# Convolution A three images ahead, the prologue's DMAs on three queues, and another order of the last convolutions

## The reference

```python
x = x + _L0_conv_ref(_gn(x), L0_conv_weights, L0_conv_biases)   # 3x3 convolution, zero padding, bias
x = x + _L1_conv_ref(_gn(x), 5)          # Newton-Schulz inverse of each 128x128 matrix, 5 iterations
x = x + _L2_conv_ref(_gn(x), L2_conv_weight)                    # 3x3 convolution, circular, by FFT
x = x + _L3_conv_ref(_gn(x), L3_conv_K)  # 3x3 convolution, last row and column set to zero
```

## Time and profile before

| | us |
|---|---|
| median of three runs | 725.62 (724.13 to 728.28) |
| the profiled execution | 727.48 |
| its span | 725.70 |
| busy: PE, weight loads | 607.9 (84%), 507.1 (70%) |
| busy: DVE, ACT, POOL | 533.2 (73%), 383.5 (53%), 198.6 (27%) |
| mean granted clock of PE | 0.954 |

### The profile page before, as it was taken

The page is one execution under the profiler, slowest core; times in us unless marked ns, Lnnn a source line. Parts: engine busy times, 40 slices in busy tenths (PEclk is TensorE's granted clock), DMA queues, the critical chain, the costliest instruction groups (busy, mean ns, idle before and its releaser), DMA issues.

```text
span 725.7 us, 11297 instructions
## 1 busy us (share of the span) xinstructions
PE 607.9 (84%) x3752; PEld 507.1 (70%) x3752; DVE 533.2 (73%) x1304; ACT 383.5 (53%) x559; POOL 198.6 (27%) x289
## 2 busy tenths in 40 slices
PE   0695679749989989899899989999999969995956
PEld 0464667748777777778778778778777858884644
DVE  3855976666796878797797779887978687648551
ACT  0351437424666566664667456656677436753632
POOL 5122023112252224231242315222423122201302
PEclk9998999969999999999999999999999998998888
DMA  5186001950379322971488334942372135222352
GB/s 152 54 106 186 1 30 34 148 182 30 90 82 268 75 81 52 158 209 44 101 85 255 86 85 71 237 121 64 75 241 53 35 80 168 53 74 70 85 132 58
DMA packets 89124, 76.43 MB, mean 105 GB/s; under 512 B 6572, under 2 KB 81228, under 8 KB 86252
## 3 DMA queue, kind: packets, MB, share of 16 engines
q1 hardware_dynamic: 87548, 74.07, 44.6%
q0 software_dynamic: 1536, 1.86, 1.0%
HBM read 38.14 MB, written 24.25 MB: 86 GB/s over the span
## 4 chain that ended last, share of the span: by engine, by line
PE 38%; DVE 35%; ACT 8%; issue 7%; SPq 7%; DMA 4%; POOL 1%; DVEq 0%; ACTq 0%
PE conv_ps L750 23%; DVE zl L1005 6%; PE z L831 3%; DVE stB L676 3%; DVE bn_D L538 2%; DVE bn_A L538 2%; PE z L833 2%; PE z L835 2%; PE z L826 2%; ACT d_A L650 2%; PE z L840 2%; ACT zh L938 2%; DVE d_C L615 2%; DMA rows_dram<-x 1%; SPq L377 1%
## 5 line engine op out<-in xcount | busy, mean ns | idle before, releaser
L1005 DVE SCALAR_TENSOR_TENSOR zl<-z,zh 128x1024 fp32r<-128x1024 f32 x128 | 154.4, 1219 | 73.4 <-ACT zh L938 70.9
L938 ACT ACTIVATE zh<-z 128x1024 fp32r<-128x1024 f32 x128 | 130.2, 1019 | 69.6 <-PE z L835 36.8
L831 PE MATMUL z<-zh 128*128 128x256 f32 x512 | 154.3, 301 | 15.2 <-DVE zl L1005 15.2
L833 PE MATMUL z<-zl,zh 128*128 128x256 f32 x512 | 146.9, 287 | 0.0
L835 PE MATMUL z<-zh,zl 128*128 128x256 f32 x512 | 146.5, 286 | 0.0
L750 PE MATMUL conv_ps<-d_A,w_D 128*96 128x512 f32 (+1 forms) x432 | 104.5, 391 | 17.3 <-DVE w_D L608 16.5
L831 PEld LDWEIGHTS z<-zh 128*128 128x128 f32 x512 | 100.1, 196 | 24.1 <-DVE zl L1005 21.0
L750 PE MATMUL conv_ps<-d_C,w_C 128*96 128x512 f32 (+1 forms) x486 | 113.9, 382 | 0.7 <-issue 0.6
L750 PE MATMUL conv_ps<-d_A,w_A 128*96 128x512 f32 (+1 forms) x378 | 95.5, 401 | 14.7 <-DVE w_A L608 10.8
L833 PEld LDWEIGHTS z<-zl,zh 128*128 128x128 f32 x512 | 100.4, 196 | 1.0
L835 PEld LDWEIGHTS z<-zh,zl 128*128 128x128 f32 x512 | 100.1, 195 | 0.0
(11 more groups left out here) (182 smaller groups left out, 899.7 us busy)
## 6 DMA issues: line engine op xcount, KB each, us to landing
x<-x_dram SPq DMA_DIRECT2D x14, 1024.0 KB, 6.6
win_C<-rows_dram SPq DMA_DIRECT2D x40, 256.0 KB, 5.5
rows_dram<-x SPq DMA_DIRECT2D x32, 256.0 KB
win_A<-x SPq DMA_DIRECT2D x48, 160.0 KB
win_D<-out_C SPq DMA_DIRECT2D x7, 1056.0 KB, 6.8
y<-out_D SPq DMA_DIRECT2D x42, 168.0 KB, 3.9
x_dram<-out_A SPq DMA_DIRECT2D x30, 192.0 KB, 2.1
win_D<-out_C SPq DMA_DIRECT2D x14, 160.0 KB, 5.8
```

Source lines behind the costliest of these rows:

```text
L831: pe.matmul(z[s][:, m, :], zh[s][:, m, 0:128], zh[s][:, m, :], start=False, stop=True, skip_group_check=True)
L833: pe.matmul(z[s][:, m, :], zh[s][:, m, 0:128], zl[s][:, m, :], start=False, stop=True, skip_group_check=True)
L938: act.activation(zh[s][:, :, :], z[s][:, :, :], ACT.Copy, scale=ROOT[j]).then_inc(s_zh[s], 1)
L1005: dve.scalar_tensor_tensor(zl[s][:, :, :], z[s][:, :, :], ROOT[j], zh[s][:, :, :].bitcast(f32), ALU.mult, ALU.subtract).then_inc(s_zl[s], 1)
```

## The change

A runs three images ahead, not two. A(2) moves from cycle 0's last slots to its slots 4 to 14, in C's tiles (`cA2`); its statistics are begun in the prologue. A(3) starts in cycle 0 (four groups) and ends in cycle 1 (two groups); cycle i then carries A(i+3), and cycles 5, 6 and 7 have no A. In cycles 5 and 6 C's six groups stand at slots 9, 11, ... 19; in cycle 7 D(5) stands at 1, 3, 5, 7, 10, 13 and the first two groups of C(6) at 16 and 20. Behind the last step come the other four groups of C(6), then C(7), D(6), D(7). C(7) writes to `out_A`, D(7) works in `win_A`, `w_A` and `out_C` (objects `cC7`, `cD7`). A(0) is now in C's tiles, A(1) in A's.

In the prologue the windows of x(0) and x(1) go out from SP, ACT and POOL, window k from queue k mod 3, with a semaphore per group, and DVE waits group by group. The same three queues copy A(0)'s rows to `x1`, and at the end store image 7's y. The image loads of x(2) and x(3) stand in SP's queue ahead of and behind those rows. The variance and Newton steps of image 0's rows stand behind the absolute sums, and norms are transposed in `spare_ps`. The waits of `high_parts`, `conv_weights` and `conv_out` are counted anew.

```diff
+        D_SLOTS, C_SLOTS, A_SLOTS = (1, 2, 3, 5, 6, 7), (9, 10, 11, 13, 14, 15), (17, 18, 19, 21, 22, 23)
+        FILL = {
+            "start": {**groups_at("A2", 4, 6, 8, 10, 12, 14), **groups_at("A", 17, 19, 21, 23)},
+            "second": {**groups_at("A3", 2, 5, first=4), **groups_at("C", *C_SLOTS), **groups_at("A", *A_SLOTS)},
+            "full": {**groups_at("D", *D_SLOTS), **groups_at("C", *C_SLOTS), **groups_at("A", *A_SLOTS)},
+            "late": {**groups_at("D", *D_SLOTS), **groups_at("C", 9, 11, 13, 15, 17, 19)},
+            "last": {**groups_at("D", 1, 3, 5, 7, 10, 13), **groups_at("C", 16, 20)},
+        }
...
         def sp_cycle(sp, i, has_D, has_C, has_A, nxt, load):
...
+            if is_int(i, 0):
+                for g in range(4):
+                    store_x1(sp, 2, g)
             store_x2(sp, i, 0)
             store_x2(sp, i, 1)
-            if has_C:
+            if has_C and not is_int(i, B - 1):
                 windows_from_windows(sp, i - 1)
                 store_y_last_row(sp, i - 1)
...
             if load:
-                load_x_rows(sp, i + 3)
+                load_x_rows(sp, i + 4)
...
         def pe_end(pe):
             i = B - 1
-            for g in range(NG):
-                conv_group(pe, cD, i - 1, g, (cC, i - 1))
+            for g in range(LAST_C, NG):
+                conv_group(pe, cC, i - 1, g)
+                if g == LAST_C:
+                    row_mean_C(pe, i)
+                if g == LAST_C + 1:
+                    row_var_C(pe, i)
+            for g in range(NG):
+                conv_group(pe, cC7, i, g)
                 if g == 0:
-                    row_mean_C(pe, i)
-                if g == 1:
-                    row_var_C(pe, i)
-            for g in range(NG):
-                conv_group(pe, cC, i, g, (cD, i - 1))
-            win_mean(pe, cD, i)
-            win_var(pe, cD, i)
-            for g in range(NG):
-                conv_group(pe, cD, i, g, (cC, i))
+                    win_mean(pe, cD, i - 1)
+                if g == 3:
+                    win_var(pe, cD, i - 1)
+            for g in range(NG):
+                conv_group(pe, cD, i - 1, g)
+                if g == 0:
+                    win_mean(pe, cD7, i)
+                if g == 2:
+                    win_var(pe, cD7, i)
+            for g in range(NG):
+                conv_group(pe, cD7, i, g)
...
         def _(sp):
...
-            for g in SP_X:
-                load_x(sp, 1, g)
-            for g in SP_ROWS:
-                rows_from_windows(sp, 0, g)
+            load_x(sp, 1, ON_SP)
             load_x_rows(sp, 2)
+            for g in range(NG):
+                rows_from_windows(sp, g, ON_SP)
+            load_x_rows(sp, 3)
...
-            store_y_rows(sp, B - 2)
+            windows_from_windows(sp, B - 2)
+            store_y_last_row(sp, B - 2)
             windows_from_windows_last(sp)
+            store_y_rows(sp, B - 2)
...
         def first_convs(dve):
...
+            win_stats_1(dve, cA2, 2, 0, 1, 2)
```

612 lines of the change are left out of this document (357 added, 255 removed).

## The result

The changed kernel takes 735.26 us in the median of four runs (734.13 to 739.39), the kernel before, run beside it, 726.95. The ratio is 1.0121 (95% interval 1.0075 to 1.0168): the change makes the kernel 1.2% slower, where 706.5 us and a gain were forecast. The profiled execution of after took 734.13 us with a span of 732.30.

A forecast was written before the change was run, and what follows sets the result against it. No engine was taken as full; each stage had its own limit: waits for loads, latency chains, weights. Terms -5.3 + 0.4 - 0.7 - 6.1 - 8.6 + 1.1 = -19.2 us gave 706.5 us, forecast 702 to 710, range 700 to 718.

The forecast's parts named there:

- Then 38.5 + 4.4 = 42.9 for the row statistics: Prologue: x1's row statistics start at 42.9, after A(1)'s low parts and A(2)'s window statistics, 4.3 us earlier than before.
- drain: Prologue rival: the window load is bound by 167 GB/s, so A(0) gains 4 us, not 6.5; 710.5 us, chance 0.17.
- its rule: Prologue: Trainium skill's rule that all issuers' DMAs share 16 engines, so several issuers save only issue time, usually small.
- One group a pair is then nearly covered: Cycle 0, first eight pairs: six groups cost 1.2 us, shorter pairs 1.5, A(2)'s weights on VectorE 1.9.
- up to 7 more were the cover gone: Cycle 0's bound: without cover in the first eight pairs, six groups would cost up to 7 us more.
- The last four pairs get one group each: Cycle 0: its last four pairs of slots take 21.2 us instead of 25.4, 4.2 less.
- The pair arithmetic: Cycles: two slots with one convolution group take 5.3 us, with two 7.4; the first group costs 1.2, the second 2.15.
- that rival: Cycles 5 and 6: D's windows come late, 3 us lost each, and C(7)'s load 2; 714.5 us, chance 0.13.
- the count of cycles by kind: Cycles 2 to 6: sorted by having A and an image load, they fall from 388.9 to 381.8 us.
- TensorE's clock: Rival: the clock falls as groups leave cycles 5 to 7, making the kernel slower; 734.5 us, chance 0.06.
- what is saved comes back: Rival: VectorE and ScalarE keep cycles as long, cycle 0 at 72, prologue without gain; 722 to 726 us, chance 0.09.
- the image load that moves other transfers: Listed sign that the forecast is wrong: an image load shifts other DMA transfers; no size given.

The follow-up runs named there:

- load3: Changed kernel, but SP issues image 3's load only after all rows of image 0 have landed in x1: 733.14 us, ratio 1.008.
- rows_first: Changed kernel, image 0's rows issued ahead of image 2's load, row means behind A(1)'s six groups, A(2)'s statistics and weights just ahead of cycle 0: 729.83 us, ratio 1.004.
- a2_no_dve: Changed kernel with computation left out: VectorE makes no statistics, mean, variance or weights for image 2: 731.34 us, ratio 1.003.
- a2_no_pe: Changed kernel with computation left out: each of A(2)'s six groups in cycle 0 is one matmul instead of nine: 734.95 us, ratio 1.011.
- move4: Changed kernel, but A(3)'s four groups of cycle 0 stand in cycle 1, which then holds all six: 735.71 us, ratio 1.014.
- ypool: Changed kernel, but POOL instead of SP issues the stores of image 6's y rows: 742.51 us, ratio 1.025.
- lastc0: Changed kernel, but all six groups of C(6) stand behind the last step, none in cycle 7: 739.07 us, ratio 1.016.
- a2w: Changed kernel, but A(2)'s mean, variance, Newton steps and weights are all made in the prologue, ahead of image 0's row statistics: 732.41 us, ratio 1.007.
- combo: Changed kernel with load3, a2w, move4, lastc0 and image 0's row means behind all six groups of A(1): 729.02 us, ratio 1.000.
- combo2: combo with VectorE's first three low parts of C(7) ahead of D(6)'s last window statistics: 722.66 us, ratio 0.997.
- bqueue: Kernel before the change with only the prologue's three queues for windows and image 0's rows added: 724.92 us, ratio 0.998.
- bqueue_5: Same kernel as bqueue, measured again in five rounds against the kernel before: 722.66 us, ratio 0.996.
- bqueue6: bqueue with the row means of image 0 moved behind all six groups of A(1): 726.34 us, ratio 1.000.

## Why the prediction was wrong

**Prologue: forecast -5.3, measured +5.75 (up to +10.3 in other executions).** The step that failed is "Then 38.5 + 4.4 = 42.9 for the row statistics". I let VectorE wait for A(1)'s low parts and for image 2's windows, which I put at 38 to 41 and which came at 45.7, and took it for granted that image 0's rows would be there. I had the load's weight in my hands (DMA share 1.27 for 13 us, with 1 MB of rows beside it) and asked only when the load would land, not what it does to the rows that share the engines. load3 and rows_first show that the load behind cost 3.4 to 7.5 us and the load ahead nearly 6, of which 2.0 is SP's later issue. A(0) gained 3.2 us, where 6.5 was the forecast: there the rival "drain" was right (it had 4, by the 167 GB/s that came in; 174 did), and its rule, which I had weighed against the trace, was the better guide in both places.

**Cycle 0: forecast +0.4, measured +13.2.** The step that failed is "One group a pair is then nearly covered ... and 1.9 for A(2)'s weights on DVE". The pairs of the first half were long before because VectorE was full: busy 14.9 of 16.4 us in slots 2 to 7. That is cover for TensorE, and none for VectorE. I charged 1.9 us for the weights and nothing for the mean, the deviations, the first and last windows, the variance and the Newton steps, which take 5.6 us from 69.3 on and 1.9 from 82.2 on; a2_no_dve gives 7.1 for all of it. The groups cost about 1 us each (a2_no_pe, 3.8 for four and 2.7 for two; move4, 1.0 to 1.25), so my 2.7 for all six (1.2 and 1.5) was short as well, and the bound that I gave ("up to 7 more were the cover gone") named the wrong engine. Together these are 13.6 of the 14.6 us by which the first eight pairs grew, where I had 4.6. "The last four pairs get one group each ... 4.2 less" failed too: they took 22.55 instead of 23.9 us, 1.35 less. The pair arithmetic had put them at 21.2 and 25.4, so a second group taken away was worth less there than its 2.15; what holds these pairs no run shows. Some of the steps also took six times as long as I had read them, see below.

**Cycle 1: forecast -0.7, measured -2.4.** ScalarE's wait for C(0)'s windows is 5.17 us (9.13 before), inside the bound.

**Cycles 2 to 6: forecast -6.1, measured -5.7** (-7.0 to -8.7 in most other runs, against a stretch that took 385.6 to 388.9 in the kernel before and its variants). No window of D was late; that rival is out, and the count of cycles by kind was the right tool.

**Cycle 7: forecast -8.6, measured -11.4,** just beyond my lower bound of 55. The pairs with one group cost less than I had put; TensorE's clock held 0.99.

**The end: forecast +1.1, measured +7.1 (most other executions +9.3).** Of the 6.0 us that it missed in the profiled execution, C(7)'s start has 2.0 (windows landed at 12, and ScalarE, VectorE and POOL need 3.2 for the first group, where I had left 1), C(7) itself about 1.2 (a first group of 3.75), D(6)'s start and length the next microsecond, and the tail 1.8: SP's last issue comes 0.8 later behind D(7)'s last group than forecast and the span's end another 1.0 behind that issue. The rows of image 6 ahead of SP's windows were in the forecast, and ypool, which took them away, made the tail 4.1 us longer; why the tail is longer stays open. The 2 us more of most other executions are D(6)'s, 16 us long instead of 14.6. Another limit of the count: four groups behind the last step stood there as if covered by TensorE's wait. lastc0 shows that two more cost 3.6 of their 4.3 us, since C(7) takes over the tiles of parts and weights from C(6) and VectorE makes D(6)'s statistics first.

**The sign.** Stage by stage the gains of cycles 1 to 7 (19.5 us) are there, and even larger than forecast (15.4). The prologue, cycle 0 and the end were forecast at -3.8 together and came at +26.1. The chance of 0.05 for slower stood by TensorE's clock alone, and the clock didn't decide it. What did was in no rival as a way to a slower kernel: the rival "what is saved comes back" named VectorE, with cycle 0 at 72 us (79.8 came) and the prologue without gain, and stopped at 726; the image load that moves other transfers stood among the signs of being wrong, without a price.

## What to carry to other kernels

Before a step is moved into a stretch because one engine has room there, read that stretch's busy time on every engine that the step uses: its small vector steps can cost more than its matmuls. A bulk load put ahead of or right behind small copies that somebody waits for delays them, whoever issues them; gate it on their landing, or put them first. And idle time of an engine ahead of a reused tile is room only as far as the wait hangs on something else: beyond that, what is put before it moves it along. Last, two fixes that fill the same wait don't add up.

## What the runs showed of the hardware

Small VectorE steps, 0.16 to 0.23 us long otherwise, took 0.96 to 1.08 us while POOL multiplied `DS` (the row at 71.51 above, and its neighbours), and the cast of `w_C` took 1.29 instead of 0.31 under POOL's low part. Four such steps in a row took 3.3 us more around the start of cycle 0. Which steps they are depends on what stands there: in a2w, a2_no_dve, combo and combo2 it is image 0's own row steps, which the change had put behind the sums; in the kernel before VectorE was idle under `DS`. So these 3.3 us came with the new order and are not in the 7.1 of a2_no_dve. In rows_first the seven window statistics ran beside `DS` in 3.25 us, as fast as elsewhere. The Trainium skill, "SBUF — State Buffer", section "SBUF: two separate sides", says that a VectorE operation with two SBUF inputs and a GpSimd operation that reads SBUF exclude each other for a whole instruction. The trace agrees for the steps with two inputs: POOL's four multiplications ran 4.04 us for four, 1.0 each, which is what each VectorE step took beside them. The cast and one of the row steps in a2w (a TENSOR_SCALAR, 0.97 us) have one input and were held as well; what held them no run here shows.

The landing of small copies beside a bulk load scattered by 4 us (54.3 to 58.4) between executions of the same prologue, which is most of the scatter of the changed kernel's prologue; with the rows first it was 43.1 to 45.1 in four (rows_first, bqueue, bqueue_5, bqueue6).
